# Four-layer graph network on one core: layer 2 scores stacked on 96 rows, layer 3 attention divided by its row sums, centred weights, and new queue orders

## Time and profile before

| | |
|---|---|
| runs | 998.18, 1001.0, 1003.43 us; median 1001.0 us |
| profiled execution, own time | 999.49 us |
| its span | 997.7 us |
| granted TensorE clock, mean over the span | 0.977 of full speed |
| busy, share of the span | PE 93%, PEld 81%, DVE 84%, POOL 75%, ACT 70% |
| DMA | 61.8 MB, 23.4% of 16 engines' time |

### The profile page before, as it was taken

How to read it: one execution, slowest core, us unless ns; L and a number is a source line. 1 busy time by engine, 2 the same in 40 slices (tenths; PEclk the granted TensorE clock), 3 DMA queues, 4 the chain that set the end, 5 groups by cost and what they waited for, 6 DMA issues and landing times. The chain is left out here.

```text
span 997.7 us, 32479 instructions
## 1 busy us (share of the span) xinstructions
PE 928.4 (93%) x11228; PEld 812.0 (81%) x11228; DVE 836.6 (84%) x2503; ACT 702.5 (70%) x1516; POOL 746.0 (75%) x1169
## 2 busy tenths in 40 slices
PE   4687899999999999999999999999999999999854
PEld 3566788888888888888888888888888888887642
DVE  4467888898998999899988899899989898988752
ACT  3445667777777777877787777787787777776552
POOL 2655768878878888888888888888888888876551
PEclk9779999999999999999999999999999999999995
DMA  7102221222222222222222222222222222212200
GB/s 238 40 9 60 58 68 50 56 54 61 71 71 71 56 68 53 58 61 61 71 71 71 59 66 56 56 59 65 68 71 71 63 63 67 54 37 52 52 20 21
DMA packets 110231, 61.80 MB, mean 62 GB/s; under 512 B 57072, under 2 KB 105840, under 8 KB 110192
## 3 DMA queue, kind: packets, MB, share of 16 engines
q1 hardware_dynamic: 110192, 61.30, 23.4%
HBM read 35.83 MB, written 8.39 MB: 44 GB/s over the span
## 5 line engine op out<-in xcount | busy, mean ns | idle before, releaser
L784 ACT ACTIVATE late<-preG,nbG,rsG 128x256 f32<-128x256 f32 x64 | 34.9, 592 | 63.1 <-POOL nbG L1295 63.1
L481 PE MATMUL bank<-z1h,W 128*128 128x256 f16 x256 | 72.0, 281 | 3.8 <-DVE z1l L951 3.6
L482 PE MATMUL bank<-z1l,W 128*128 128x256 f16 x256 | 72.0, 281 | 0.0
L483 PE MATMUL bank<-z1h,W 128*128 128x256 f16 x256 | 72.0, 281 | 0.0
L1374 POOL TENSOR_TENSOR late<-late,Smx 128x512 f32<-128x512 f32 x64 | 67.5, 1055 | 4.7 <-DVE Smx L1182 4.7
L481 PE MATMUL bank<-W,rFh 128*128 128x256 f16 x256 | 70.7, 276 | 0.0
L483 PE MATMUL bank<-W,rFl 128*128 128x256 f16 x256 | 70.7, 276 | 0.0
L482 PE MATMUL bank<-W,rFh 128*128 128x256 f16 x256 | 70.7, 276 | 0.0
L1300 POOL TENSOR_TENSOR gp<-late,bdb 128x512 f32<-128x512 f32 x32 | 40.7, 1271 | 32.7 <-ACT late L897 32.7
L813 ACT ACTIVATE r<-bank,b1c 128x256 f32<-128x256 f32 x128 | 52.6, 463 | 16.7 <-PE bank L483 16.7
L1283 POOL TENSOR_TENSOR y0l<-y,y0h 128x512 f16<-128x512 f32 x32 | 37.2, 1163 | 31.6 <-ACT y0h L766 31.6
(11 more groups left out here) (286 smaller groups left out, 4519.0 us busy)
## 6 DMA issues: line engine op xcount, KB each, us to landing
Vbd<-vst SPq DMA_DIRECT2D x128, 66.0 KB, 2.1
xin<-x SPq DMA_DIRECT2D x32, 256.0 KB, 2.7
xres<-x SPq DMA_DIRECT2D x32, 256.0 KB, 2.9
Kbd<-kst SPq DMA_DIRECT2D x128, 64.0 KB, 2.0
out<-late SPq DMA_DIRECT2D x32, 256.0 KB, 2.2
mrow<-mask SPq DMA_DIRECT2D x32, 128.0 KB, 3.1
atA<-adj_t SPq DMA_DIRECT2D x64, 32.0 KB, 2.3
aC<-adj SPq DMA_DIRECT2D x64, 32.0 KB, 2.1
```

Source lines behind the costliest of these rows:

```text
L481: pe.matmul(o, sh, mh, start=start, stop=False, skip_group_check=True)
L482: pe.matmul(o, sh, ml, start=False, stop=False, skip_group_check=True)
L483: return pe.matmul(o, sl, mh, start=False, stop=stop, skip_group_check=True)
L784: m = act.activation(dst[:, t], pre[k][:, t], ACT.Identity, bias=nb[k][:, t:t + 1], scale=rs[k][:, t:t + 1])
```

## The change

Layer 2's scores: no Kbd. q and k go out to DRAM and come back with each head's 32 columns on rows 0 to 31, three times below one another: q as (high, high, low) and k as (high, low, high), 96 rows in all. One product of 96 rows per head, tile and graph (64 stationary and 64 moving columns) takes the place of the three. Output rows are stored one step later, and SP's order is another.

```
+        q_by_head = [nc.dram_tensor(f"q_by_head{i}", (2, P, 2 * TOK), F16).ap() for i in range(2)]
+        k_by_head = [nc.dram_tensor(f"k_by_head{i}", (2, P, 2 * TOK), F16).ap() for i in range(2)]
...
-        Kbd = sb("Kbd", [P, 4, 2, 2, TOK], F16)
+        Qs = sb("Qs", [96, 2, 4, 2, TOK], F16)
+        Ks = sb("Ks", [96, 4, 2, TOK], F16)
...
+            def park(name, dram, at):
+                sp.dma_start(dram[at.par].rearrange("l p k -> p l k"),
+                             (qst if name == "q" else kst)[:].rearrange("p l c k -> p l (c k)")
+                             ).then_inc(ev(name + "_parked"), 16)
+            def fetch(name, dram, dst, parts, at):
+                sp.wait_ge(ev(name + "_parked"), at.chain(16, 16)).then_inc(ev("sp_held"), 1)
+                for r, hl in enumerate(parts):
+                    sp.dma_start(dst[32 * r:32 * r + 32].rearrange("p a c k -> p a (c k)"),
+                                 dram[at.par][hl].rearrange("(a p) k -> p a k", p=32)
+                                 ).then_inc(ev(name + "_stacked"), 16)
...
                 at = At(3, j, s)
                 if there(at):
-                    place_k(at)
+                    park_k(at)
                 for k, load in enumerate(loads):
                     at = At(k, j, s + 1)
-                    if load and there(at):
+                    if load and k != 5 and there(at):
                         load(at)
+                    at = At(3, j, s)
+                    if k == 0 and there(at):
+                        fetch_k(at)
+                    at = At(5, j, s - 1)
+                    if k == 0 and there(at):
+                        store(at)
...
                     place_v(at)
-                at = At(5, j, s)
+                at = At(2, j, s)
                 if there(at):
-                    store(at)
+                    park_q(at)
+                at = At(5, j, s + 1)
+                if there(at):
+                    load_layer3(at)
+                at = At(2, j, s)
+                if there(at):
+                    fetch_q(at)
...
                     for c in range(2):
-                        for i, (qq, hl) in enumerate(((qh, 0), (qh, 1), (ql, 0))):
+                        for a in range(4):
                             for b in range(2):
                                 tok = slice(t * P + 64 * b, t * P + 64 * b + 64)
-                                m = pe.matmul(o[64 * b:64 * b + 64, c * 256:(c + 1) * 256], qq[:, c, tok],
-                                              Kbd[:, :, hl, c, tok], start=(i == 0), stop=(i == 2),
+                                h = 4 * c + a
+                                m = pe.matmul(o[64 * b:64 * b + 64, h * NODES:(h + 1) * NODES],
+                                              Qs[:, at.par, a, c, tok], Ks[:, a, c, tok], start=True, stop=True,
                                               skip_group_check=True)
```

```
+                for b in range(2):
                     for k in range(2):
-                        m = mm3(bG[:, tok], Qh[:, k, tok], Ql[:, k, tok], Qh[:, k, tok], Ql[:, k, tok], k == 0, k == 1)
+                        for i, (qa, qb) in enumerate(((Qh, Qh), (Qh, Ql), (Ql, Qh))):
+                            for t in range(TILES):
+                                tok = slice(t * P + 64 * b, t * P + 64 * b + 64)
+                                m = pe.matmul(bG[64 * t:64 * t + 64, D + b * NODES:D + (b + 1) * NODES], qa[:, k, tok],
+                                              qb[:, k, tok], start=(k == 0 and i == 0), stop=(k == 1 and i == 2),
+                                              skip_group_check=True)
...
+                pe.transpose(bG[:, D + P:2 * D], SAs[:].rearrange("p b k -> p (b k)"), ident[:]
+                             ).then_inc(ev("attn_turned"), 1)
...
+                pe.wait_ge(ev("attn_lo"), at.n())
+                pe.matmul(bG[:].rearrange("p (t d) -> p t d", t=TILES), ones16[:, 0:1].broadcast_to([P, P]),
+                          blr[:].rearrange("p (o d) -> p o d", o=1).broadcast_to([P, TILES, D]), start=True, stop=False,
+                          skip_group_check=True)
+                for t in range(TILES):
+                    m = project_tm(bG[:, t * D:(t + 1) * D], xgFh, xgFl, Wr, t, onto=True)
                 m.then_inc(ev("o2_raw"), 1)
-                    pe.matmul(bG[:, t:t + 1], SAh[:, t], ones16[:, 0:1], start=True, stop=False, skip_group_check=True)
...
+                for t in range(TILES):
+                    for i, (sa, y) in enumerate(((SAh, y3h), (SAh, y3l), (SAl, y3h))):
+                        for b in range(2):
+                            rows = slice(64 * b, 64 * b + 64)
+                            m = pe.matmul(bG[rows, t * D:(t + 1) * D], sa[rows, t], y[rows, t], start=False,
+                                          stop=(i == 2), skip_group_check=True)
                 m.then_inc(ev("o1"), 1)
...
+                    m = dve.tensor_tensor_reduce(SA[:, b], bG[:, D + b * NODES:D + (b + 1) * NODES], atG[:, at.par, b],
+                                                 1.0, 0.0, ALU.mult, ALU.add, bG[:, b:b + 1])
...
+                dve.scalar_tensor_tensor(out=pre["G"][:].rearrange("p t k -> p (t k)"), in0=bG[:], scalar=0.0,
+                                         in1=x3[:, at.par].rearrange("p t k -> p (t k)"), op0=ALU.max, op1=ALU.add
+                                         ).then_inc(ev("preG"), 1)
...
+                pool.tensor_tensor(SAs[:], SA[:], srec[:].rearrange("p (t o) -> p t o", o=1).broadcast_to(
+                    [P, TILES, NODES]), ALU.mult).then_inc(ev("attn_scaled"), 1)
```

The rest: the rows of Wv1 and Wo and the bias bo are centred while they are set up, so the inputs of norms C and F have mean zero, `rstd` leaves out L1295 for them and `norm` the bias; the second half of rFl (L1077) goes from DVE to POOL; three factors are folded into neighbours; `rmm` and three small columns are read from PSUM in place of SBUF; Kbd's four memsets go; and all ORDER, HEAD and TAIL lists are new:

```
+CENTRED = "CF"
+ORDER_PE = [3, 2, 3, 1, 0, 2, 4, 4, 5, 4, 2, 1, 0, 5, 0, 2, 5, 3, 3, 0, 1, 0, 5, 4, 1, 2, 3, 5, 5, 2, 3, 1, 0, 0, 4]
+ORDER_DVE = [0, 0, 2, 0, 0, 0, 2, 0, 3, 1, 4, 4, 0, 4, 0, 4, 0, 4, 2, 2, 3, 1, 0, 1, 5, 1, 5, 0, 2, 5, 2, 5, 3, 2, 5, 4, 3, 1, 3, 3, 4, 4, 5, 4, 2, 1, 5, 5, 2, 5, 1, 0, 0, 0, 1, 3, 3, 4]
```

More of the change, by code:

```diff
@@ L129, in build @@
         x3, x4 = [v.rearrange("p a (t d) -> p a t d", t=TILES) for v in (x3, x4)]
-        cx, gw, xg, o2, o3 = [late[1][:, i] for i in range(5)]
+        cx, gw, xg = [late[1][:, i] for i in range(3)]
         Sm, Ssb = [v.rearrange("p t (h k) -> p t h k", h=HEADS) for v in (Sm, Ssb)]
@@ L464, in _ @@
                     step(j, par)
-            for s in range(last, STEPS):
+            for s in range(last, STEPS + 1):
                 step(None, s)
@@ L498, in project_tm @@
                     m = mm3(o, ah[:, k, tok], al[:, k, tok], W[:, 0, k, n0:n0 + n], W[:, 1, k, n0:n0 + n],
-                            k == 0, k == chunks - 1)
+                            k == 0 and not onto, k == chunks - 1 and not onto)
                 return m
@@ L754, in stream5 @@
-                pe.wait_ge(ev("row_scale"), at.chain(2, 1))
-                for t in range(TILES):
-                    m = mm3(bG[:, t * D:(t + 1) * D], SAh[:, t], SAl[:, t], y3h[:, t], y3l[:, t], True, True)
+                    for i, (sa, y) in enumerate(((SAh, y3h), (SAh, y3l), (SAl, y3h))):
[3 more added lines that the diff above has]
+                                          stop=(i == 2), skip_group_check=True)
@@ L774, in set_up @@
                         act.wait_ge(ev("setup"), 4)
+                    elif name in ("Wv1", "Wo"):
+                        act.wait_ge(ev("centring"), 3 if name == "Wv1" else 6)
                     else:
@@ L965, in _ @@
             dve.memset(ones16[:], 1.0).then_inc(ev("const"), 1)
-            for buf in (atG, wpad, same):
+            for buf in (wpad, blf, same):
                 dve.memset(buf[:], 0.0).then_inc(ev("const"), 1)
@@ L977, in part, with centre @@
                     low(W[:, 1], split_from[name], W[:, 0], WS).then_inc(ev("unstaged"), 1)
+                def centre(rows, sums, done):
+                    dve.tensor_reduce(wmean[:, sums], rows, AX.X, ALU.add).then_inc(ev("centring"), 1)
+                    dve.wait_ge(ev("centring"), done + 1)
+                    dve.tensor_scalar(wmean[:, sums], wmean[:, sums], -1.0 / D, None, ALU.mult
+                                      ).then_inc(ev("centring"), 1)
+                    dve.wait_ge(ev("centring"), done + 2)
+                    for i in range(rows.shape[1]):
+                        k = sums.start + i
+                        m = dve.tensor_scalar(rows[:, i], rows[:, i], wmean[:, k:k + 1], None, ALU.add)
+                    m.then_inc(ev("centring"), 1)
                 dve.wait_ge(ev("w2_in"), 64)
@@ L1235, in stream5 @@
+                m.then_inc(ev("attn"), 1)
                 yield
[L1236 to L1241 removed]
@@ L1246, in stream5 @@
                 yield
-                dve.wait_ge(ev("o1"), at.n())
-                dve.wait_ge(ev("row_scale"), at.chain(2, 2))
-                if at.earlier(1):
-                    dve.wait_ge(ev("o3_relu"), at.n(-1))
-                for t in range(TILES):
```

(10 more changed lines are left out.)

220 lines of the change are left out of this document (115 added, 105 removed).

## The result

| | before | after |
|---|---|---|
| median of the timed runs | 1000.11 us (998.18 to 1003.43) | 969.74 us (968.26 to 972.53) |
| ratio, 95% interval | | 0.967 [0.963, 0.970] |
| profiled execution, own time and span | 999.49, 997.7 us | 970.12, 968.3 us |
| mean granted clock | 0.977 | 0.981 |
| DMA | 61.8 MB, 23.4% | 95.3 MB, 35.2% |

What follows compares the result with a forecast made beforehand. PE, busy without holes, was taken to set the 28.00 us step by its sum. 26 x (-0.86 + 0.1) = -19.8 and +1 for the ends gave 980.7, median 982 us; range 967 to 1004 us.

Steps and rivals of the forecast that it cites:

- The term for the loop: Steady steps: 26 steps, each -0.86 us from PE's sum and +0.1 for waiting on K, -19.8 us in all.
- The term for the ends: Pipeline's filling and emptying: longer K trip against less norm and attention work, +1 us, between -6 and +8.
- Scores, s3 and their shape: PE, layer 2's scores and s3: smaller paired products sharing one shape change, 1.11 us in place of 2.42, -1.31 a step.
- o1: PE's o1: 12 products of 256 columns; +0.22 us a step if the two graphs pair, +0.87 if not; +0.22 taken.
- o1 does not pair: Rival at o1 on PE: products sharing a bank run one after the other, +0.65 us a step, 999 us; chance 0.12.
- K's way: K's trip through DRAM: lands at 12.2 us after the K projection starts, scores reached at 12.15; charged +0.1 us a step.
- K comes late: Rival at PE's wait ahead of tile 0's scores: K 1.55 us late each step, 1022 us; chance 0.14.
- The loop's length: Steady part of the kernel before: counted as 26 steps at 28.0 us, 728 us of the 997.7 us span.
- means of C and F: POOL: the means of norms C and F go, about 1.1 us less work a step, with no gain in the step.
- Stores a step later cost nothing: SP's queue: the store, one step later, waits for a norm that is long done; costs nothing.
- The attention chain costs nothing: From s3 to o2 across engines: some 2.5 us of work while PE has other pieces until about 19.5; costs nothing.
- new wait: Rival at DVE: SAl behind seven full instructions, so o2 waits about 0.5 us a step, 995 us; chance 0.14.

Runs made afterwards that it cites:

- fetch_later: Changed kernel with SP's three fetches of K issued behind the output's store, the residual's load and layer 2's load: 1027.7 and 1034.3 us.
- old_tail: Changed kernel with the order lists of the kernel before in the 5 last steps: ratio 0.992 to the kernel before.
- before_new_tail: Kernel before, pieces unchanged, with the changed kernel's order lists in its last four steps: 1015.7 us, ratio 1.018 to the kernel before.
- store_now: Changed kernel with the output stored in its own step, last in SP's queue: 975.4 us, ratio 0.979 to the kernel before.
- o1_serial: Changed kernel with o1's loop over the two graphs outside the loop over the three parts: ratio 0.970 to the kernel before.

## Why the prediction was right and where it was wrong

It had the mechanism (PE's sum sets the step) and the side, but forecast 982 us where 970 was measured. Two steps failed. The term for the loop, 26 x (-0.86 + 0.1) = -19.8, measured -25.8: the wait for K that it charged is not there, and PE's sum and the start of the loop gave more. The term for the ends, +1, measured -3.6: it priced the ends by instructions and left the new HEAD and TAIL lists and the clock at nothing. The remaining 2 us of the miss are the median's distance from the profiled execution, put at +1.5 and measured at -0.4. By its own steps:

- **Scores, s3 and their shape**, forecast 1.11 us: 1.10. **o1**, +0.22 if it pairs: 0.87 in place of 0.65, +0.22. **Bias** 0.22: 0.23; **turn** 0.11: 0.11. Sum -0.86, as forecast. The rival "o1 does not pair" is refuted by 0.87 us (1.52 if not) and by the starts 3 ns apart. The rule of the Trainium skill (TensorEngine Tiling (Array Packing), Restrictions and Gotchas), that different row tiles can't use one PSUM bank at one time, is not borne out by `o1`'s rows: the two graphs' products differ in input rows, write one bank and run in pairs.
- **The rest of PE's sum**, not in the forecast: the step of before was 27.97 (28.08 and 27.85 by turns) and is 27.00, so -0.97. Added up over all distances of one step, the other 0.11 lies in many small changes of place, none over 0.1 (z1 2.71 to 2.63, layer 1's two-column products 0.20 to 0.14). 25 x 0.11 = 2.8 us.
- **K's way, charged 0.1 us a step (2.6 in all)**: nothing. K is there at 11.7 after the K projection begins, not 12.2. k_lo ended at 4.6 (4.8 forecast); the issues are what was mis-sized: 1.30 us for the three fetches (0.43 each), where I took 0.62 from DMAs of 64 KB of which four stand in a row. The landings, 2.2 and 2.5, were right (2.2 and 2.4). PE was at the scores at 12.1, as forecast (12.15). So the margin is 0.4 us, and fetch_later shows what lies beyond it; by that run the rival "K comes late" is too cheap, since the lower clock adds a third.
- **The loop's length.** 26 steps at 28.0 by the forecast. 25 took 701.4 us, 28.05 each: two of them, near the loop's start, are 29.2 and 29.0, 2.3 us above the pitch (PE waits 1.1 and 0.9 us for HBl in them), where the new kernel has 0.6 (27.6 in its first). That too was not in the sum. Together 25 x 0.97 + 2.3 - 0.6 = 25.9 (25.8 measured); forecast 19.8. The term "26 x (-0.86 + 0.1)" is thus 6 us too small, and this is the first half of the miss.
- **The ends, forecast +1**: -3.6, and the second half of the miss (4.6). That it lies within the given -6 to +8 is luck, since two larger errors of opposite sign make it up. The parts were not seen rightly, and its "-1.6 for the rest" comes from no row. K's longer trip is there: group 31's scores come 11.6 us after its K projection, in place of 8.7 (+2.9; forecast +2.7). But filling lost 6.3 and emptying gained 9.9. Where that gain is, the chain of before shows:

```profile
944.03 0.85 PE bank L677 x12
947.64 0.70 DVE preF L1210
...
952.03 0.51 POOL nbF L1295 x2
...
953.07 0.58 ACT late L784
953.66 0.53 ACT E L884
```

  Before, the last group's second E starts 9.6 us after its first scores. It stands behind norm F of the group ahead in ACT's list, and that norm waits for its mean on POOL (nbF). After, norm F also stands ahead of E, but its input is made before these scores begin (preF at 923.03) and it needs no nbF. The two E start at

```profile
927.64 1.05 POOL late L1454
928.72 0.64 ACT E L942
...
931.16 0.63 ACT E L942
```

  The scores begin at 925.5, so the second E comes 5.7 us later. From there to the end it is 53.7 us before and 42.8 after. How much of this is the order and how much the missing mean, no run at this place separates. I had counted instructions at the ends, not the order; and I knew the new HEAD and TAIL lists and did not follow them. old_tail and before_new_tail show that the TAIL lists are worth 23 us with the new pieces, 12.6 of them in PE's busy time at the lower clock, and -17 with the old.
- **"Cost nothing", means of C and F**: right for C, wrong for F (0.35 a step), very wrong for both (1.6). This did not hurt the forecast's number, since the forecast is of the kernel that leaves them out; but counting them as less work on an engine with room missed the point: without this edit, in these lists, the change is slower than before, 1.018. In these lists it is worth 1.6 us a step, more than any term of PE's sum (-1.31 for `s3` and the scores), and the prediction passed it by.
- **Stores a step later cost nothing**: right in the step (27.0 either way in store_now). **The attention chain costs nothing**: right with these lists, no wait of PE for `SAl` in the loop; in the old lists 8.2 us of 300. So the "new wait" rival had a true place and the order keeps it away.
- Of its signs, those on the pieces, on PE's wait for Ks (under 5 us: 1.9) and on the landings held; the pitch, 27.0, is just under the 27.1 to 27.3 that it gave. DVE 23.66 (24 forecast), POOL 20.5 (21.6).

**Open**: where the last 0.9 us of both means together come from; why the new pieces need 12.8 us more in the fill in the old lists (the trips, the centring and the longer attention were not separated); what lowers the clock more in one emptying than in another with the same lists. None of the versions beats the changed kernel.

## What to carry to other kernels

Where one engine has no hole, its sum by distances between starts gives the step to 0.1 us, but it holds only for an order in which everything arrives: with the order of before, the same pieces cost 12% instead of saving 3%. So check every stretch of a helper engine by itself. POOL is idle for a quarter of the step, yet one stretch of it has 0.34 us of slack towards PE and a few short waits inside: 0.7 us ahead of these waits cost nothing, 0.7 us behind them 0.35 a step. A wait of PE can be paid twice, once as a wait and once at the lower clock that follows (fetch_later: 44.5 and 15.5 us). At the pipeline's ends the order of the work weighs more than the instructions; follow the last group's chain through the new lists before giving the ends a number.

## What the runs showed of the hardware that was not expected

- Products on two 64 x 64 tiles of the array run as pairs even where two others stand between them in PE's program: in o1_serial they start 10 ns apart, and 12 of them take 0.66 us without the shape change, as they do side by side.
- A pair's price goes by its moving columns: 0.108 us at 256 (96 or 128 rows) and 0.031 at 64 (96 rows in the scores, 128 in `s3`), both at a clock of 1.00.
- In fetch_later, where PE waits 1.2 to 4.2 us once a step, the granted clock fell to 1.2 GHz in 8 of 25 steps (mean 0.94 over such a step, 0.90 over the first): 30.4 to 30.8 us and 33.6, in place of 28.3 to 29.2.
- The issue of a DMA on SP takes 0.38 to 0.43 us for `k_by_head`, `xin` and Ks, but 0.62 for each of four to Kbd and 0.72 for each to atA (1.44 for two); bytes don't explain it (256 KB in 0.38, 64 KB in 0.62), and no run tells what does.
- The median landing of Ks rose from 2.5 to 2.9 us in fetch_later, where the store and two loads are issued right ahead of it.
